# Conditioning in four column tiles of the TensorE array, loads in a new order on two queues, VectorE's early program in another order

## What is computed

```python
B, S, D, E = 16, 256, 256, 128          # B batches; H = 4 * E = 512
def _layer_norm(x, gamma, beta, eps=1e-05):
    mean = jnp.mean(x, axis=(-2, -1), keepdims=True)
    var = jnp.mean(jnp.square(x - mean), axis=(-2, -1), keepdims=True)
    return (x - mean) * jax.lax.rsqrt(var + eps) * gamma + beta
emb = 5000.0 * t[:, None] * freqs[None, :]
h = jnp.concatenate([jnp.sin(emb), jnp.cos(emb)], axis=1)
h = jax.nn.silu(h @ W1 + b1)            # 128 -> 512
h = h @ W2 + b2                         # 512 -> 512
scale = (h @ Wsc + bsc)[:, None, :]     # 512 -> 256
shift = (h @ Wsh + bsh)[:, None, :]
out = jax.nn.silu(scale * _layer_norm(x, gamma, beta) + shift)
out = out @ W_in + b_in
out = jax.nn.silu(scale * _layer_norm(out, gamma, beta) + shift)
return out @ W_out + b_out + x
```

## Time and profile before

| | |
|---|---|
| median of 3 runs | 103.71 us (102.8 to 103.94) |
| profiled execution | span 101.5 us from its first to its last instruction; no other time of it is given, and the 2.2 us up to the median are what lies around the span |
| TensorE busy | 88.8 us, 88% |
| VectorE busy | 80.9 us, 80% |
| ScalarE busy | 58.1 us, 57% |
| GpSimd busy | 39.7 us, 39% |
| moved by DMA | 11.89 MB, with loads up to about 24 us |

### The profile page before, as it was taken

The page is one execution under the profiler, slowest core; times in us unless marked ns, Lnnn a source line. Parts: engine busy times, 40 slices in busy tenths (PEclk is TensorE's granted clock), DMA queues, the critical chain, the costliest instruction groups (busy, mean ns, idle before and its releaser), DMA issues.

```text
span 101.5 us, 1109 instructions
## 1 busy us (share of the span) xinstructions
PE 88.8 (88%) x267; PEld 41.3 (41%) x268; DVE 80.9 (80%) x197; ACT 58.1 (57%) x174; POOL 39.7 (39%) x40
## 2 busy tenths in 40 slices
PE   5995999989999999976579995995998699999990
PEld 2351173365355544224243352451643245444450
DVE  1510617999979989999999899999799967789951
ACT  5030024244774898397679149939952999966600
POOL 1000027359244069039972992950493020120000
PEclk9999999985589999999985999999999999999999
DMA  0799999993000000000005000500500050230484
GB/s 4 146 354 399 374 384 397 397 408 150 0 3 0 0 3 0 0 0 0 0 0 207 0 0 0 207 0 0 185 28 3 0 207 0 85 125 0 159 300 161
DMA packets 6598, 11.89 MB, mean 117 GB/s; under 512 B 960, under 2 KB 2752, under 8 KB 6592
## 3 DMA queue, kind: packets, MB, share of 16 engines
q1 hardware_dynamic: 6592, 11.82, 32.4%
HBM read 7.63 MB, written 4.19 MB: 116 GB/s over the span
## 4 chain that ended last, share of the span: by engine, by line
DVE 41%; PE 31%; POOL 8%; DMA 7%; issue 5%; ACT 4%; SPq 2%; DVEq 0%; ACTq 0%
PE big L581 21%; DVE act L413 8%; DVE act L421 7%; DMA x_sb<-x_dram 7%; DVE bn L338 5%; DVE act L383 5%; DVE act L374 4%; DVE act L366 3%; POOL act L222 3%; POOL act L225 3%; DVE o_sb L429 3%; DVE wrow L389 2%; ACT squares L275 2%; PE big L550 2%; ACT act L257 2%
## 5 line engine op out<-in xcount | busy, mean ns | idle before, releaser
L257 ACT ACTIVATE act<-act,cond 128x256 f32<-128x256 f32 x64 | 35.7, 590 | 19.8 <-DVE act L421 11.3
L581 PE MATMUL big<-act,win_sb 128*128 128x512 f32 x64 | 33.2, 644 | 0.9 <-DVE act L413 0.8
L581 PE MATMUL big<-act,wout_sb 128*128 128x512 f32 (+1 forms) x68 | 31.0, 605 | 2.0 <-DVE act L413 1.8
L581 PEld LDWEIGHTS big<-act,wout_sb 128*128 128x128 f32 x68 | 12.9, 198 | 15.1 <-issue 11.4
L581 PEld LDWEIGHTS big<-act,win_sb 128*128 128x128 f32 x64 | 11.9, 204 | 12.9 <-issue 9.7
L222 POOL TENSOR_TENSOR act<-act,gamma_sb 128x512 f32<-128x512 f32 x10 | 13.7, 1382 | 7.7 <-DVE act L366 7.7
L275 ACT ACTIVATE squares<-big,shift 128x256 bf16<-128x256 f32 x32 | 15.0, 470 | 1.9 <-PE big L581 0.7
L225 POOL TENSOR_TENSOR act<-act,beta_sb 128x512 f32<-128x512 f32 x10 | 15.0, 1510 | 0.5
L421 DVE SCALAR_TENSOR_TENSOR act<-act,rstd,beta_sb 128x512 f32<-128x512 f32 x16 | 14.5, 949 | 0.1
L229 POOL TENSOR_TENSOR rstd<-var,minus_half 128x2 f32<-128x2 f32 x8 | 5.9, 733 | 22.1 <-DVE var L402 22.1
L338 DVE BATCH_NORM_STATS2 bn<-x_sb 128x6 f32<-128x512 f32 x16 | 10.2, 680 | 4.6 <-DMA x_sb<-x_dram 4.6
(11 more groups left out here) (56 smaller groups left out, 64.5 us busy)
## 6 DMA issues: line engine op xcount, KB each, us to landing
x_sb<-x_dram SPq DMA_DIRECT2D x8, 512.0 KB, 10.7
out_dram<-o_sb SPq DMA_DIRECT2D x15, 256.0 KB, 2.1
w_sb<-w_dram SPq DMA_DIRECT2D x1, 1024.0 KB, 6.0
wss_sb<-wsc_dram SPq DMA_DIRECT2D x1, 512.0 KB, 7.8
wss_sb<-wsh_dram SPq DMA_DIRECT2D x1, 512.0 KB, 8.8
w_sb<-w_dram SPq DMA_DIRECT2D x1, 256.0 KB, 2.7
gamma_sb<-gamma_dram SPq DMA_DIRECT2D x1, 256.0 KB, 8.9
beta_sb<-beta_dram SPq DMA_DIRECT2D x1, 256.0 KB, 8.5
```

What stands on the lines that cost most here:

```text
L257: return nc.scalar.activation(buf[:, c, b], buf[:, c, b], ACT.Silu, bias=cond[:, 1, c, i:i + 1], scale=cond[:, 0, c, i:i + 1], **kw)
L581: mm = nc.tensor.matmul(acc[:, c, b * S:(b + n) * S], w[:, k, c * P:(c + 1) * P], act_in[:, k, b:b + n].rearrange("p b s -> p (b s)"), sta ...
```

## The change

- The two products with 16 stationary columns and 512 moving ones become `rows_product`: for each k, four products of 32 stationary columns (16 batches and 16 columns of zeros) and 128 moving ones, each with its own `tile_position`, a column tile of the array. The result lies in all 128 partitions. ScalarE copies it with one instruction, and `transposed` is one product with a pick matrix of 64 columns. GpSimd clears h1 and h2 for the zero columns (semaphore `pads_set`).
- t, enc and bias are loaded from ScalarE's queue; SP's order is w1, x[0], w2, gamma, x[1], beta, Wsc, Wsh, W_in and the rest as before.
- `mean1(0)` and `mean1(1)` stand ahead of the rows products, not inside. The warm products around the transposing go; six stand behind `mean1(1)`.
- `mean1(2)` and `variance1(2)` go from ahead of the Y loop into its step 0 (`CHAIN_OF_STEP`).
- wsum becomes one reduction on VectorE. The angle's last two steps become one, with the phase added as ScalarE's bias.
- VectorE's early program is in another order.

```diff
-CHAIN_OF_STEP = {1: 3, 3: 4, 5: 5}
+CHAIN_OF_STEP = {0: 2, 1: 3, 3: 4, 5: 5}
-WARM_AFTER = 4
-WARM_BETWEEN = 2
+WARM_BEFORE_HIDDEN = 4
+WARM_BEFORE_COND = 6
...
-            sp.dma_start(t_sb[:], t.rearrange("(a b) -> a b", a=1).to_broadcast([P, B])).then_inc(t_in, 16)
-            sp.dma_start(enc_sb[:], enc).then_inc(enc_in, 16)
-            sp.dma_start(bias_sb[:], biases).then_inc(bias_in, 16)
             sp.dma_start(w1_sb[:], w1).then_inc(w1_in, 16)
+            load_x(0)
             sp.dma_start(w2_sb[:], w2.rearrange("(k p) n -> p k n", p=P)).then_inc(w2_in, 16)
-            load_x(0)
+            sp.dma_start(gamma_sb[:], gamma).then_inc(gamma_in, 16)
+            load_x(1)
+            sp.dma_start(beta_sb[:], beta).then_inc(beta_in, 16)
...
+            nc.gpsimd.memset(h1[:], 0.0).then_inc(pads_set, 1)
+            nc.gpsimd.memset(h2[:], 0.0).then_inc(pads_set, 1)
...
+            act.dma_start(t_sb[:], t.rearrange("(a b) -> a b", a=1).to_broadcast([P, B])).then_inc(t_in, 16)
+            act.dma_start(enc_sb[:], enc).then_inc(enc_in, 16)
+            act.dma_start(bias_sb[:], biases).then_inc(bias_in, 16)
...
-                for i in range(2):
-                    half = slice(i * H // 2, (i + 1) * H // 2)
-                    nc.scalar.activation(rows[:, half], acc[0:B, 1, half], ACT.Identity).then_inc(rows_ready, 1)
+                nc.scalar.activation(rows[:], acc[:, 1, 0:P], ACT.Identity).then_inc(rows_ready, 1)
...
+            dve.wait_ge(win_in, 16)
+            nc.vector.tensor_reduce(wsum[:], win_sb[:], AX.X, ALU.add).then_inc(wsum_ready, 1)
...
+            def rows_product(acc, h, w):
+
+                for k in range(KH):
+                    for j in range(KH):
+                        mm = nc.tensor.matmul(acc[j * ROWS:(j + 1) * ROWS, 1, 0:P], h[:, k], w(k, j),
+                                              start=(k == 0), stop=(k == KH - 1), tile_position=(0, j * ROWS))
                 return mm
+
+            def transposed(acc, rows):
+
+                return nc.tensor.matmul(acc[:, 0, 0:KH * B], rows[:], enc_sb[:, COL_PICK:COL_PICK + KH * B],
+                                        start=True, stop=True)
...
-            warm(4)
+            warm(WARM_BEFORE_HIDDEN)
+            pe.wait_ge(consts_set, 1)
+            mean1(0)
...
+            rows_product(big[1], h1, lambda k, j: w2_sb[:, k, j * P:(j + 1) * P]).then_inc(h2_rows_mm, 1)
             variance1(0)
-            transposed(big[1], h2_rows, h2_rows_ready).then_inc(h2_mm, 1)
+            pe.wait_ge(h2_rows_ready, 1)
+            transposed(big[1], h2_rows).then_inc(h2_mm, 1)
...
+            mean1(1)
+            warm(WARM_BEFORE_COND)
+            variance1(1)
             pe.wait_ge(h2_ready, 1)
...
+            rows_product(big[2], h2, lambda k, j: wss_sb[:, k, j // C, (j % C) * P:(j % C + 1) * P]).then_inc(cond_rows_mm, 1)
+            pe.wait_ge(cond_rows_ready, 1)
+            transposed(big[2], cond_rows).then_inc(cond_mm, 1)
```

More of the change, by code:

```diff
@@ L82, in build @@
         h0 = sb("h0", [P, B])
[L83 to L86, removed]
+        h1 = sb("h1", [P, KH, ROWS])
+        h2 = sb("h2", [P, KH, ROWS])
+        h2_rows = sb("h2_rows", [P, P])
+        cond_rows = sb("cond_rows", [P, P])
         cond = sb("cond", [P, 2, C, B])
@@ L444, in _ @@
             stats1(1)
+            weigh_beta(0)
             stats1_deviation(1)
-            weigh_gamma(0)
-            weigh_beta(0)
+            weigh_gamma(1)
             stats1_variance(1)
-            stats1(2)
+            centre1(1)
+            weigh_beta(1)
             dve.wait_ge(cond_mm, 1)
@@ L454, in _ @@
                                     ALU.add).then_inc(cond_ready, 1)
-            centre1(1)
-            stats1_deviation(2)
-            weigh_gamma(1)
+            dve.wait_ge(win_in, 16)
+            nc.vector.tensor_reduce(wsum[:], win_sb[:], AX.X, ALU.add).then_inc(wsum_ready, 1)
             dve.wait_ge(mean_b_mm, 1)
             nc.vector.tensor_scalar(mean_b[:], stat2[:, 0:1], 1.0 / C, None, ALU.mult).then_inc(mean_b_ready, 1)
-            dve.wait_ge(wsum_ready, C)
+            dve.wait_ge(wsum_ready, 1)
             nc.vector.tensor_scalar(wmean[:], wsum[:], float(P) / (S * D), None, ALU.mult).then_inc(wmean_ready, 1)
@@ L465, in _ @@
                                     ALU.subtract).then_inc(b_in_c_ready, 1)
-            weigh_beta(1)
-            stats1_variance(2)
+            stats1(2)
             dve.wait_ge(wmean_ready, 1)
@@ L470, in _ @@
             mean2_partial(0)
+            stats1_deviation(2)
+            mean_shift2(0)
             stats1(3)
-            mean_shift2(0)
+            stats1_variance(2)
             centre1(2)
-            stats1(4)
-            mean2_partial(1)
             weigh_gamma(2)
             weigh_beta(2)
+            mean2_partial(1)
+            stats1(4)
             stats1_deviation(3)
@@ L624, in _ @@
             mm.then_inc(h1_mm, 1)
-            warm(4)
+            warm(WARM_BEFORE_HIDDEN)
+            pe.wait_ge(consts_set, 1)
+            mean1(0)
             pe.wait_ge(h1_ready, KH)
             pe.wait_ge(w2_in, 16)
-            pe.wait_ge(consts_set, 1)
-            for k in range(KH):
-                mm = nc.tensor.matmul(big[1][0:B, 1], h1[:, k], w2_sb[:, k], start=(k == 0), stop=(k == KH - 1))
-                if k == KH - 1:
-                    mm.then_inc(h2_rows_mm, 1)
-                if k == 2:
-                    mean1(0)
+            rows_product(big[1], h1, lambda k, j: w2_sb[:, k, j * P:(j + 1) * P]).then_inc(h2_rows_mm, 1)
             variance1(0)
-            transposed(big[1], h2_rows, h2_rows_ready).then_inc(h2_mm, 1)
+            pe.wait_ge(h2_rows_ready, 1)
+            transposed(big[1], h2_rows).then_inc(h2_mm, 1)
             pe.wait_ge(bias_in, 16)
@@ L645, in _ @@
             pe.wait_ge(wsh_in, 16)
-            for k in range(KH):
-                mm = nc.tensor.matmul(big[2][0:B, 1], h2[:, k], wss_sb[:, k].rearrange("p a n -> p (a n)"),
-                                      start=(k == 0), stop=(k == KH - 1))
-                if k == KH - 1:
-                    mm.then_inc(cond_rows_mm, 1)
-                if k == 1:
-                    mean1(1)
-            variance1(1)
-            transposed(big[2], cond_rows, cond_rows_ready).then_inc(cond_mm, 1)
-            mean1(2)
-            warm(WARM_AFTER)
-            variance1(2)
+            rows_product(big[2], h2, lambda k, j: wss_sb[:, k, j // C, (j % C) * P:(j % C + 1) * P]).then_inc(cond_rows_mm, 1)
+            pe.wait_ge(cond_rows_ready, 1)
+            transposed(big[2], cond_rows).then_inc(cond_mm, 1)
             pe.wait_ge(win_in, 16)
@@ L696 @@
     enc = np.zeros((P, N_ENC), np.float32)
-    enc[:B, COL_EYE:] = np.eye(B, dtype=np.float32)
+    for j in range(KH):
+        enc[j * ROWS:j * ROWS + B, COL_PICK + j * B:COL_PICK + (j + 1) * B] = np.eye(B, dtype=np.float32)
     enc[:, COL_FREQ] = np.tile(freqs, 2)
@@ L700 @@
     enc[half:, COL_PHASE] = math.pi / 2
+    enc[:, COL_LOW] = -PI_BELOW - enc[:, COL_PHASE]
+    enc[:, COL_HIGH] = PI_BELOW - enc[:, COL_PHASE]
     arrays = {
```

42 lines of the change are left out of this document (14 added, 28 removed).

## The result

The changed kernel takes 113.16 us (median of 4 runs, 112.94 to 114.9) against 103.41 us (4 runs, 102.8 to 103.94) for the kernel before: ratio 1.0969, interval 1.0876 to 1.1063. It is 9.7% slower. The forecast was 102.7, the range ended at 106.0, and no rival reached the result. The profiled execution spans 111.1 us, its mean clock is 0.877 (before 101.5 and 0.950).

The account below looks back on a forecast made before the run. It took the kernel as a start-up, a nearly gapless VectorE program of about 60 us and a TensorE tail; -0.35 - 0.46 - 0.2 = -1.0 us on 103.7 gave 102.7 us (own range 101.9 to 103.5; overall 100.4 to 106.0).

Parts of the forecast that it names:

- Transfers: Start-up loads: bulk starts 1.37 us earlier, w2 lands at 8.55, x[0] about 5.9; small loads 0.3 us later (0 to 0.7).
- Two rows products: Conditioning's two products as column tiles: 1.8 us each if only different tiles overlap, ends 1.0 and 3.4.
- rival A: Rows products: all passes side by side, 1.0 us instead of 1.8, twice, -1.6 on cond; 101.1 us, chance 0.22.
- rival B: Rows products: tiles do not overlap, 3.4 us instead of 1.8, twice, +3.2 on cond; 105.9 us, chance 0.18.
- The walk to cond: Step-by-step times of the start, from x[0]'s statistics to cond: cond at 19.75 us, 1.85 earlier than before.
- VectorE's program passes a shift at deviation(3) on unchanged: From deviation(3) VectorE's program is unchanged, so its shift (32.85 against 33.20 us, 0.35 earlier) carries to the end.
- the idle 1.5 us that the walk had foreseen: Y loop, behind stats1(3): VectorE idles 1.5 us until the power of group 2's variance is ready.
- Rival C: TensorE's clock falls in the gap before x[1] is averaged: cond +2.0, 104.7 us, tail to 106.5; chance 0.24.

Follow-up runs that it names:

- e13: Changed kernel with t alone laid out by the host as 128 rows, still three small loads on ScalarE's queue: 110.01 us, ratio 1.0586.
- e2: Kernel before with only the change's loads (t, enc, bias on ScalarE's queue, SP's loads in the new order): 108.36 us, ratio 1.0527.
- e3: Kernel before with only the column tiles, one copy, one transposing product and cleared padding; loads and order as before: 103.33 us, ratio 1.0034.
- e6: Changed kernel with t, enc and bias merged into one load of 128 rows on ScalarE's queue: 108.77 us, ratio 1.0507.
- e10: Changed kernel with one merged small load, stats1(4) early, group 2's mean and variance ahead of Y0, stats1(2) in group 1's variance wait: 103.4 us, ratio 0.993.
- e12: Kernel before with column tiles, SP's loads in the new order and one merged small load on ScalarE's queue: 100.94 us, ratio 0.9817.

## Why the prediction was wrong

**Transfers: the step that failed first.** The prediction adds 0.3 us (0 to 0.7) to the small loads for sharing the engines with w1, and gives the bulk the full 1.37 us of its earlier issue. Measured: enc lands 4.0 us later than before (7.5 against 1.18 + 2.3 = 3.5), and w2 at 10.15 instead of 8.55. The reason that the runs show is mutual: three loads of 128 rows each beside bulk packets are served slowly and hold all transfers together at 98 to 158 GB/s in the same time (2 to 5 us). About 2 us of it, for enc as for x[0], is the reading of one row of DRAM by all 128 partitions (e13), and one load of 128 rows costs its reader only 0.5 to 0.9 us (2.8 to 3.2 against 2.3). The bound of 0.7 had no row behind it; the trace before has no stretch in which small and bulk packets run together from the beginning. Alone, in the old order, this step is worth 5.3% (e2). The Trainium skill, "DMA: Bandwidth & Descriptors", section "Issuing engines are not separate DMA queues", says that transfers of all issuing engines run on the same 16 engines and interleave, so that a second queue saves issue time only; the traces agree: 1.37 us of issue time were saved, and against them stand 4.0 of landing lost. The same page's rules for kernel authors ask for many small transfers to be made one, and the merged load agrees: 4.4 us by the medians. Of these, 3.2 come already with t in rows of its own (e13, 110.01), with the loads as many as before.

**Two rows products: the size was that of rival A.** I took 1.8 us, with only different tiles side by side, and kept 1.0 and 3.4 as ends. At the full clock 32 passes take 1.08, about 26 ns from one to the next ((1.08 - 0.27) / 31, where 0.27 is the duration of one pass there), 49 at the low clock ((1.93 - 0.42) / 31). Rival A's 1.0 was right and rival B is out; that A would also bring 1.6 us was not. By the Trainium skill, "TensorE: Matmul & The Clock Gate", Part 3, packed products span one product's time and some 4 ns for each further tile. For four groups of four tiles that is an estimate of 4 x (2 x 0.107 + 3 x 0.004) = 0.90 us, and the 1.08 of the trace, which includes the whole 0.27 of the last pass, is close; the other statement of that part, that loads overlap only with another row group, the trace contradicts, since 32 loads of 32 columns went by within these 1.08 us with all rows in use. None of it was worth anything alone (ratio 1.0034): ahead of the first `centre1` the next term, the statistics of x[0], was late, and behind it the clock was lower (e3).

**The walk to cond: its time held where the loads were right, its terms did not.** With the merged load cond was ready at 20.25 against 19.75, with a clock of 0.66 from 10 to 20 us where the walk had the full one: a product too dear and a clock too high, which cancelled. The walk's last terms (18.6, and 0.32, 0.35, 0.2 and three times 0.15) also add up to 19.92 and not to the 19.75 that it carries on.

**"VectorE's program passes a shift at deviation(3) on unchanged": failed, and the walk to it missed a wait.** The walk follows VectorE and asks what VectorE waits for. It never asks what TensorE waits for: `stats1(4)` ended on it at 31.3 + 1.5, and I took that as the start of deviation(3), without noting that `mean1(3)` stands between the two halves of Y1 and holds the second half up. By the walk's own times (variance1(2) to 26.2, four passes 1.7 or more) TensorE was through the first half by about 28 and idle for over 4 us; it is 4.96. The order rows ahead of the prediction show the move of `stats1(4)` behind gamma and beta, so this could have been seen. `stats1(4)` early takes off 5.0 us (107.49 against 112.48), or 4.6 in the pair with the merged load (104.19 against 108.77), but not all of that is the missed wait, since the edit also fills the idle 1.5 us that the walk had foreseen (0.56 and 0.82 here). What the walk missed is 0.74 us of VectorE's waiting for `mean1(3)` and 2.07 for the variance of group 3, 2.8 in sum; 1.7 of the 2.07 is Y1's second half at the low clock (3.67 instead of 1.96). The 2.07 lie behind deviation(3), in the stretch that I held constant (70.7 us instead of 68.3).

**Rival C: happened, and in two places more.** I let the clock fall in the gap from 11.9 to 14.1 us. In the changed kernel it stood at 0.50 already at 10 us, behind the 3.16 us in which TensorE waited for the late sine, and again at Y0 and at Y1. With the merged load, where the sine was prompt, it fell in just the gap that the rival names: TensorE was idle for 2.51 us up to 14.02, and the clock was at 0.50 from 12 us (e6). So the forecast's full clock would have failed with good loads too. Filling gaps with zeros gives back 3.5 to 3.8 us of it. I gave this rival up to +3.8 (106.5), with no other loss; together with the other two steps it is over the range.

The parts aren't additive: loads alone +5.3%, tiles alone 0, order alone about +9% at prompt loads (+7% by the fastest executions), together +9.7%. That a late start hides part of the waits of the order would explain it, but no run shows this by itself. Not tried apart: wsum on VectorE, and group 2's place alone; they share the 3.3 us between 104.19 and 100.94 with the rest of the order. Open as well is why the kernel with group 2 ahead of Y0 (e10) stays 2.5 us above e12 by the medians (1.0 by the fastest executions) and scatters; in its profile w2 landed 8.5 us after issue (7.2 in e12) and the clock was low for 16 us, which may be cause or effect.

## What to carry to other kernels

A second queue saved issue time and no more: small loads that something waits for go ahead of the bulk, or are packed into one load with a row per partition, rather than one row that all partitions read. When work moves on one engine, walk every engine's program, and for each product between two others ask when its operand is made; a small product in mid-stream is a barrier for all behind it. A gap on TensorE can be paid for twice, by its length and by the lower clock of the products that come after it, so that a shorter product can bring on the low clock that takes its gain. Shortening an operation is worth nothing until what follows it is ready.
